# Attention probabilities turned by VectorE and DMA instead of TensorE, and weighed two tiles later

## What is computed

```python
xn = layernorm(x)                                   # x: (2, 1024, 512)
q, k, v = xn @ Wq.T, xn @ Wk.T, xn @ Wv.T           # 32 heads of q, 8 of k and v, 128 wide
q, k = rmsnorm(q, q_norm_w), rmsnorm(k, k_norm_w)
scores = q @ k.T / sqrt(128) + slope[head] * (key - query), -1e30 where key > query
s = (softmax(scores) @ v) @ Wo.T
g = silu((silu(xn @ w_gate.T) * (xn @ w_up.T)) @ w_down.T)   # 1376 inner columns
out = x + s * g
```

## Time and profile before

| | before |
|---|---|
| median of 3 runs | 2454.9 us (2453.91 to 2457.38) |
| the profiled execution: its time | 2455.46 us |
| the profiled execution: its span | 2453.7 us |
| TensorE busy | 99% of the span |
| VectorE, ScalarE, GpSimd busy | 69%, 50%, 31% |
| DMA moved | 92.19 MB, mean 38 GB/s |
| mean granted clock of TensorE | 0.998 of full speed |

### The profile page before, as it was taken

One profiled execution on the slowest core, in us unless ns is written; L12 is line 12 of the kernel. 1 busy time (PEld: TensorE's weight loads), 2 busy tenths in 40 slices (PEclk: granted clock), 3 DMA queues, 4 the chain that ended last, 5 costly groups with the idle time before them and its releaser, 6 DMA issues.

```text
span 2453.7 us, 37432 instructions
## 1 busy us (share of the span) xinstructions
PE 2422.6 (99%) x13232; PEld 2070.7 (84%) x13232; DVE 1693.7 (69%) x3788; ACT 1236.1 (50%) x2548; POOL 756.9 (31%) x2053
## 2 busy tenths in 40 slices
PE   7999999999999999999999999999999999999998
PEld 6888888888888888878888888888888888888887
DVE  7777777777778787823377787777777777777132
ACT  4555554555545555543355555555555545545333
POOL 2323231413233323244522232323232314131443
PEclk9999999999999999999999999999999999999999
DMA  3010000000000000023320101010000000010232
GB/s 130 1 40 4 27 18 27 18 27 18 27 18 27 18 27 18 27 91 125 112 78 1 44 1 44 1 44 1 27 18 26 18 27 18 1 44 14 90 103 103
DMA packets 23289, 92.19 MB, mean 38 GB/s; under 512 B 6592, under 2 KB 6720, under 8 KB 19136
## 3 DMA queue, kind: packets, MB, share of 16 engines
q1 hardware_dynamic: 23104, 89.80, 10.5%
HBM read 85.60 MB, written 4.19 MB: 37 GB/s over the span
## 4 chain that ended last, share of the span: by engine, by line
PE 96%; DVE 2%; ACT 1%; issue 1%; POOL 0%; DMA 0%; DVEq 0%; ACTq 0%; POOLq 0%
PE out_ps L401 17%; PE score_ps L377 16%; PE out_ps L414 14%; PE qkv_ps L351 14%; PE ring_ps L388 10%; PE qkv_ps L352 7%; PE score_ps L504 5%; PE qkv_ps L504 4%; PE ring_ps L520 4%; PE ring_ps L359 2%; PE out_ps L520 1%; PE ring_ps L364 1%; PE score_ps L351 0%; DVE y L997 0%; DVE xT_lo L868 0%
## 5 line engine op out<-in xcount | busy, mean ns | idle before, releaser
L597 ACT ACTIVATE pT_hi<-ring_ps 128x512 fp32r<-128x512 f32 x576 | 344.0, 599 | 509.8 <-PE ring_ps L388 497.2
L818 DVE TENSOR_TENSOR pT_lo<-ring_ps,pT_hi 128x512 fp32r<-128x512 f32 x576 | 396.8, 690 | 90.6 <-ACT pT_hi L597 86.0
L589 ACT ACTIVATE probs<-probs,low_min 128x896 f32<-128x896 f32 (+7 forms) x512 | 395.2, 774 | 50.4 <-DVE low_min L810 50.1
L1016 POOL TENSOR_SCALAR rs_x<-sq_sum 128x5 f32<-128x5 f32 x122 | 24.8, 203 | 1128.1 <-DVE sq_sum L749 1128.1
L388 PE MATMUL ring_ps<-ident,probs 128*128 128x128 f32 x2304 | 345.6, 273 | 0.0
L388 PEld LDWEIGHTS ring_ps<-ident,probs 128*128 128x128 f32 x2304 | 281.7, 140 | 42.1
L810 DVE CUSTOM_DVE_ANT_0 probs<-score_ps,rel_sb,slope 128x512 f32<-128x512 f32 (+5 forms) x504 | 301.7, 599 | 5.7 <-PE score_ps L377 4.3
L377 PE MATMUL score_ps<-kv_hi,qT_hi 128*128 128x320 f32 (+4 forms) x760 | 275.6, 363 | 3.0 <-DVE xT_lo L868 2.0
L401 PE MATMUL out_ps<-pT_hi,kv_hi 128*128 128x512 f32 x576 | 265.8, 461 | 2.9 <-DVE pT_lo L818 2.6
L377 PE MATMUL score_ps<-kv_hi,qT_lo 128*128 128x320 f32 (+4 forms) x760 | 261.0, 343 | 0.0
L377 PE MATMUL score_ps<-kv_lo,qT_hi 128*128 128x320 f32 (+4 forms) x760 | 260.3, 342 | 0.0
(11 more groups left out here) (178 smaller groups left out, 5293.5 us busy)
## 6 DMA issues: line engine op xcount, KB each, us to landing
qkv_raw<-w_ffn_dram SPq DMA_DIRECT2D x44, 768.0 KB, 4.2
qkv_raw<-w_qkv_dram SPq DMA_DIRECT2D x15, 1536.0 KB, 6.9
o_raw<-w_o_dram SPq DMA_DIRECT2D x16, 1024.0 KB, 4.8
o_raw<-x_dram SPq DMA_DIRECT2D x4, 1024.0 KB, 6.7
out_dram<-y SPq DMA_DIRECT2D x16, 256.0 KB, 3.7
probs<-x_dram SPq DMA_DIRECT2D x3, 1024.0 KB, 7.9
qkv_raw<-w_qkv_dram SPq DMA_DIRECT2D x4, 384.0 KB, 6.6
probs<-x_dram SPq DMA_DIRECT2D x2, 512.0 KB, 4.8
```

The lines of the kernel that those rows point to most:

```text
L589: act.activation(row, row, ACT.Exp, scale=-1.0, bias=low_min[:, i % 2, h, HEAD_CHUNKS[i] - 1:HEAD_CHUNKS[i]], accum_out=row_sum[:, i % 2, ...
L597: act.activation(pT_hi[:, n % SLOTS, :], ring_ps[:, ring_bank(r), :], ACT.Copy).then_inc(ring_high, 1)
L818: dve.tensor_tensor(out=pT_lo[:, n % SLOTS, :], in0=ring_ps[:, ring_bank(r), :], in1=pT_hi[:, n % SLOTS, :].bitcast(F32), op=ALU.subtract) ...
```

## The change

- The probabilities are no longer turned by TensorE. `turn_blocks` on VectorE turns them in place by blocks of 32x32 right behind the exponentials. SP writes the whole tile to a DRAM tensor (`turn_probs` on SP), waits until it is there, and reads it back (`probs_home`) by four DMAs for each group of up to four key tiles, each DMA filling 32 partitions, in runs of up to 2 KB. That places the blocks, so the tile arrives transposed in `pT`, which has two group buffers.
- There is one `probs` buffer (before: two), in an order by blocks of 32, so the first `bias` of a tile waits until the write of the previous tile has landed. `rel_sb` is laid out to match. The chunks of scores are now of 4 key tiles and the rest (before: equal halves), in three banks.
- The tile of queries i - 2 is weighed in step i, in one run after the scores, and its output is projected in step i + 1.
- `divide` is gone. The reciprocals travel through DRAM too (`rec_out_at`), come back as a row on all partitions, and `scale_att` (VectorE) multiplies the weighed output by them.
- `high_probs` and `low_probs` read SBUF instead of PSUM; 6 of the 36 low parts of a unit go to GpSimd (`POOL_LOWS`), and so does `low_att`, now with both inputs in SBUF.
- ScalarE squares and sums q and k in five instructions with accumulators (`squares`); VectorE's sum is gone.
- TensorE still turns q and k, into the bank that they were projected to. The scale of q and k is applied to k instead of q.
- SP's queue gets, for each tile, one write, the write of the reciprocals (4-byte pieces), the row's return, and four or eight DMAs back.

The core of the diff (the indentation is cut by 8; lines that only serve the first tiles are left out):

```diff
+GROUP = 4
...
+HIGH_SLOTS, LOW_SLOTS = 4, 3
+SBANKS = 3
...
+POOL_LOWS = {4: (2, 4), 5: (2, 4), 6: (3,), 7: (3,)}
...
-probs = [sb("probs0", [P, G, S - P]), sb("probs1", [P, G, S])]
...
+probs = sb("probs", [P, G * S])
+pT_hi, pT_lo = sb("pT_hi", [P, HIGH_SLOTS, G * P], F32R), sb("pT_lo", [P, LOW_SLOTS, G * P], F32R)
+pT, att = sb("pT", [P, 2, GROUP * G * P]), [sb("att0", [P, G * P]), sb("att1", [P, G * P])]
...
+turned_out = nc.dram_tensor("turned_out", (2, P, TILES * G * P), F32).ap()
+rec_out_at = nc.dram_tensor("rec_out_at", (2, G, P), F32).ap()
...
+def keys_of(i, part):
+    return part * GROUP, min((part + 1) * GROUP, i + 1)
...
+    def turn_probs(U, i):
+        t = tile(U, i)
+        slot = t % 2
+        alone(probs_turned, t * G)
+        if t > 2:
+            back = (U - (i < 2)) * GROUPS + GROUP_AT[(i - 2) % TILES + 1]
+            for k in range(2):
+                alone(probs_back[k], (back + 1 - k) // 2 * BLOCKS * 16)
+        sp.dma_start(turned_out[slot, :, 0:(i + 1) * G * P], probs[:, 0:(i + 1) * G * P]).then_inc(probs_out, 16)
+        alone(rec_done, t)
+        if t > 2:
+            alone(rec_back[slot], (t - 1) // 2 * 16)
+        sp.dma_start(rec_out_at[slot].rearrange("g p -> p g"), rec[:, i % 2, :], allow_slow_non_contiguous=True).then_inc(rec_out, 16)
+    def probs_home(U, i):
+        t = tile(U, i)
+        slot = t % 2
+        alone(probs_out, t * 16)
+        for part in range(GROUPS_IN[i]):
+            lo, hi = keys_of(i, part)
+            group = U * GROUPS + GROUP_AT[i] + part
+            if group >= 2:
+                done = chunks_to_group(group - 2)
+                alone(low_by_dve, done // TURNS * DVE_LOW_AT[TURNS] + DVE_LOW_AT[done % TURNS])
+                alone(low_by_pool, done // TURNS * POOL_LOW_AT[TURNS] + POOL_LOW_AT[done % TURNS])
+            there = turned_out[slot].rearrange("(a r) n -> r a n", a=BLOCKS)
+            run = (hi - lo) * G * SQUARE
+            for k in range(BLOCKS):
+                at = lo * G * P + k * run
+                sp.dma_start(pT[k * SQUARE:(k + 1) * SQUARE, group % 2, 0:BLOCKS * run]
+                             .rearrange("r (a n) -> r a n", a=BLOCKS), there[:, :, at:at + run]).then_inc(probs_back[group % 2], 16)
...
+    def rec_home(U, i):
+        t = tile(U, i)
+        slot = t % 2
+        alone(rec_out, t * 16)
+        if t > 2:
+            alone(att_split, t - 2)
+        sp.dma_start(att[i % 2][:, :], rec_out_at[slot:slot + 1].rearrange("a g p -> a (g p)").to_broadcast([P, G * P])
+                     ).then_inc(rec_back[slot], 16)
...
+        def attention(U, first, last):
+            for i in range(TILES):
+                loads(U, i, last)
+                if not (first and i == 0):
+                    rec_home(U - (i == 0), (i - 1) % TILES)
+                turn_probs(U, i)
+                if i == TILES - 3 and U + 1 < B * UNITS:
+                    alone(rq_done, (U + 1) * TILES)
+                    load_inv((U + 1) % UNITS)
+                if i == TILES - 1 and not last:
+                    load_slope((U + 1) % UNITS)
+                probs_home(U, i)
+                if last and i == TILES - 1:
+                    rec_home(U, i)
...
...
+        if not (first and n < SBANKS):
+            pe.wait_ge(biased, U * SCORES + n - SBANKS + 1)
+        k_hi, k_lo = k_by_block
+        for q, kt in ((qT_hi, k_hi), (qT_hi, k_lo), (qT_lo, k_hi)):
+            mm = pe.matmul(score_all[n % SBANKS][:, 0:(hi - lo) * P].rearrange("p (b j r) -> p b j r", b=BLOCKS, r=SQUARE),
+                           q[:, i % 2, h * P:(h + 1) * P], kt[:, :, lo:hi, :],
+                           start=(q is qT_hi and kt is k_hi), stop=(q is qT_lo))
...
-    def turn_probs(U, i, j, first):
-
-        r, p = RING_AT[i] + j, (i - 1) % TILES
-        ring_free(U, r, first)
-        for h in range(G):
-            if j == 0:
-                pe.wait_ge(divided, (U * TILES + i - 1) * G + h + 1)
-            tr = pe.transpose(ring_ps[:, ring_bank(r), h * P:(h + 1) * P],
-                              probs[p % 2][:, h, j * P:(j + 1) * P], ident[:, :])
-        tr.then_inc(ring_full, 1)
...
+        if not (last and i >= TILES - 2):
+            project(U + (i + 2) // TILES, (i + 2) % TILES, first and i + 2 < TILES)
+        if not (last and i >= TILES - 1):
+            turn_qk(U + (i + 1) // TILES, (i + 1) % TILES, first and i + 1 < TILES)
...
+        chunks = G * HEAD_CHUNKS[i] if i < TILES else 0
+        sooner = 2 if last and i == TILES - 2 else 0
+        for k in range(sooner):
+            scores(U, i, k, first)
+        if not (first and i <= LAG):
             out_project(U, i)
+        for k in range(sooner, chunks):
+            scores(U, i, k, first)
...
+        if not (first and i < LAG) and i < TILES + LAG:
+            V, p = U - (i < LAG), (i - LAG) % TILES
+            for j in range(p + 1):
+                weigh(V, p, j, None if first and i == LAG else U * TILES + i - LAG)
...
+    def squares(U, i, first):
...
+        for h in range(G + 1):
+            ins = act.activation(qk[i % 2][:, h * P:(h + 1) * P], acc[:, h * P:(h + 1) * P], ACT.Square,
+                                 accum_out=sq_sum[:, i % 2, h:h + 1])
+        ins.then_inc(summed, 1)
...
+            V, p = U - (i < LAG), (i - LAG) % TILES
+            highs = [] if i >= TILES + LAG or first and i < LAG else list(range(p + 1))
+            for j in highs[:HIGH_SLOTS]:
+                high_probs(V, p, j)
+            highs = highs[HIGH_SLOTS:]
+            N, n = U + (i + 1) // TILES, (i + 1) % TILES
+            if not (last and i >= TILES - 1):
+                high_q(N, n, first and n)
+                if n:
+                    high_k(N, n, first)
+            if not (last and i >= TILES - 2):
+                squares(U + (i + 2) // TILES, (i + 2) % TILES, first and i + 2 < TILES)
+                stage_v(U + (i + 2) // TILES, (i + 2) % TILES, first and i + 2 < TILES)
...
+            if i == TILES - 3 and U + 1 < B * UNITS:
+                act.wait_ge(qkv_in, (U + 1) * 16)
+                for c in range(DC):
+                    high_w(U + 1, c)
+            if i == LAG:
+                high_o(U, 0, not first)
+                high_o(U, 1, not first)
+            if i < TILES:
+                for h in range(G - 1):
+                    exp(U, i, h)
+                for j in highs[:1]:
+                    high_probs(V, p, j)
+                highs = highs[1:]
+                exp(U, i, G - 1)
+                if i == TILES - 1 and not last:
+                    high_k(U + 1, 0, False)
...
+            for j in highs:
+                high_probs(V, p, j)
...
-    def divide(U, i):
-
-        dve.wait_ge(exped, (U * TILES + i + 1) * G)
-        dve.reciprocal(rec[:, :], row_sum[:, i % 2, :]).then_inc(rec_done, 1)
-        dve.wait_ge(rec_done, U * TILES + i + 1)
-        for h in range(G):
-            row = probs[i % 2][:, h, 0:(i + 1) * P]
-            dve.tensor_scalar(row, row, rec[:, h:h + 1], None, ALU.mult).then_inc(divided, 1)
...
+    def turn_blocks(U, i, h):
+        dve.wait_ge(exped, (tile(U, i) - 1) * G + h + 1)
+        row = by_head[:, h, 0:(i + 1) * BLOCKS, :]
+        dve.transpose(row, row).then_inc(probs_turned, 1)
...
+    def scale_att(U, i):
+        t = U * TILES + i - LAG
+        dve.wait_ge(weighed, (t - 1) // TILES * TURNS + TURN_AT[(t - 1) % TILES + 1])
+        dve.wait_ge(rec_back[t % 2], ((t - 1) // 2 + 1) * 16)
+        scaled = att[(t - 1) % 2][:, :].rearrange("p (g a n) -> p g a n", g=G, a=BLOCKS)
+        dve.tensor_tensor(out=scaled, in0=out_ps[:, :].rearrange("p (a g n) -> p g a n", g=G, a=BLOCKS), in1=scaled,
+                          op=ALU.mult).then_inc(att_scaled, 1)
...
+            if not (first and i <= LAG):
+                scale_att(U, i)
+            N, n = U + (i + 1) // TILES, (i + 1) % TILES
+            if not (last and i >= TILES - 1) and not (first and i == 0):
+                scale_qk(N, n, first and n)
+            V, p = U - (i < LAG), (i - LAG) % TILES
+            lows = [] if i >= TILES + LAG or first and i < LAG else [j for j in range(p + 1) if not on_pool(p, j)]
+            for j in lows:
+                if j < LOW_SLOTS:
+                    low_probs(V, p, j)
+            lows = [j for j in lows if j >= LOW_SLOTS]
             if first and i == 0:
+                early_norms(tile(U, 2))
...
+            if not (last and i >= TILES - 1):
+                low_q(N, n, first and n)
+                if n:
+                    low_k(N, n, first)
+            chunks = G * HEAD_CHUNKS[i] if i < TILES else 0
+            sooner = 2 if last and i == TILES - 2 else 0
+            for k in range(sooner):
+                bias(U, i, k)
+            if not (first and i <= LAG):
+                if first and i == LAG + 1:
                     dve.wait_ge(y_free, b + 1)
+                    dve.memset(y[:, TILES - LAG - 1:TILES, :], 0.0).then_inc(y_zero, 1)
```

(41 more changed lines are left out.)

616 lines of the change are left out of this document (249 added, 367 removed).

## The result

| | before | after |
|---|---|---|
| median of the runs | 2454.4 us | 3357.1 us |
| profiled execution, span | 2453.7 us | 3349.5 us |
| one unit, the one shown | 127.7 us | 186.4 us |
| one unit, mean of six in the first row | 127.7 us | 183.6 us |
| TensorE busy, mean granted clock | 99%, 1.00 | 73%, 0.86 |

The changed kernel takes 1.369 times as long (95% interval 1.363 to 1.374). "Slower" was the likelier side of the forecast. Its 2505 us missed by 852 us, and the time is far outside the range.

The account below looks back on a forecast made before the run. TensorE alone was taken to set the pace (99% busy). Steps of 126.8 us plus 3.5 for the port give 130.3 a unit, 2.6 over 127.7; times 16 is 42, plus 8 for row ends: 2505 us, range 2370 to 2650.

Parts of the forecast that it names:

- first biases wait for the write: Step 7 of a unit: the previous tile's write lands at 9.7 us, first bias wanted 8.4, adding 1.3 us.
- step 3: Fourth step of a unit: output projection waits for GpSimd's low_att from 4.8 to 7.8 us; step takes 14.8 us.
- step 0: First step of a unit: 15.4 us, as a GpSimd low part stands behind the norms; this covers the write's delay.
- DMA: Transfers on SP's queue: 2.6 us for each MB plus 2.2 fixed, reciprocals counted as 0.26 MB coming back.
- Rival (2): Returns into 32 partitions run at half rate, 8.6 us a unit more, kernel 2643 us; chance 0.22.
- The port: VectorE and GpSimd block each other on two-SBUF-input instructions: 3.5 us a unit, between 0 and 8.
- The order in a step: TensorE stands for late VectorE and GpSimd work within steps 0 to 7 of a unit; steps sum to 126.8 us.
- rivals (1): VectorE's stretch is shorter, turns at the division's rate, no GpSimd blocking: unit 122.5 us, kernel 2380 us; chance 0.24.
- (3): A block turn on VectorE takes twice the assumed value: some 14 us a unit, kernel 2729 us; chance 0.06.
- TensorE's own work: TensorE's matmuls in a unit without the transposes of probabilities: 111.4 us, 16.2 us a unit removed.
- rival (4): The gain comes in full, with TensorE still the last to finish: kernel 2204 us; chance 0.05.
- Ends of a row: Extra time at the start and end of each of two rows: 4 us each, 8 in all.

Follow-up runs that it names:

- recT: Changed kernel, whole, with only the reciprocals turned on VectorE into rows and written in 16 pieces of 128 bytes: 2831.4 us.
- recT_free: Changed kernel with reciprocals as 128-byte rows, return order 0, 2, 1, 3, tile writes sourced from a never-overwritten buffer and VectorE's wait dropped: 2688.6 us.
- tinyT: Changed kernel with reciprocals as 128-byte rows, and each tile's write and returns cut to 128 bytes of each partition: 2588.4 us.
- quietT: `tinyT` with GpSimd's subtractions (low parts) made on an eighth of their columns: 2461.6 us.
- rec16: Changed kernel with reciprocals written to DRAM in 128 pieces of 16 bytes instead of 512 of 4, then read strided: 2906.8 us.
- rec16_wide: Changed kernel with 16-byte reciprocal pieces and each return filling all 128 partitions, block placement left out: 2793.2 us.
- noturnT: `quietT` with each VectorE turn cut to one block of 32 columns instead of a row: 2361.9 us.

## Why the prediction was wrong, by its own steps

The miss of 852 us, by differences of two kernels each, the later causes still in (16 units):

| step | the sum had | measured | from |
|---|---|---|---|
| reciprocals' trip | 0 beyond 0.26 MB | 526 us | after - `recT` |
| first biases wait for the write | 21 us (1.3 a unit) | 143 us (8.9) | `recT` - `recT_free` |
| the rest of the traffic (returns and slopes late) | 0 | 100 us (6.3) | `recT_free` - `tinyT` |
| GpSimd's subtractions, by the port or late | 56 us (3.5) and 48 us (3.0, step 3) | 127 us (7.9) | `tinyT` - `quietT` |

The four rows come to 896 us where the sum had 125, which is 771 of the 852. The other 82 are `quietT` against the 2380 us that the sum leaves without traffic, port and step 3's wait for GpSimd. (The sum has a delay by GpSimd in step 0 as well, not given by itself.)

**The step that failed.** "DMA", in its sentence "0.26 of reciprocals". I priced this transfer by its bytes, on its way home, and left its way out at nothing. 2 KB in 512 dense pieces is 62% of the miss. No row of the trace before has such pieces, so the term should have been bounded from both sides, as the turn's was. It was a cost of zero without a reason.

**Rival (2) was the right mechanism, too small a chance and incomplete.** "The returns run at half rate" is seen at 212 GB/s. Its price was 138 us over the forecast. The half rate by itself is worth 114 us (`rec16` - `rec16_wide`), and TensorE stands nearly as it said, 4.3 and 3.4 us ahead of the scores in a unit of `recT`. The sum's own 1.3 us for the first biases was too small besides. By its 2.6 us for each MB and 2.2 fixed, the 3.67 MB from -1.1 us on land at 10.6 and not at 9.7, which is a slip of 0.9 us a unit. The rival also left out two waits: the weighing two tiles behind waits for late returns, and the 2 KB of slopes queue behind a 2 MB write. I had written that in step 0 "the same delay is covered by GpSimd's low part"; the slopes' wait of 68 to 159 us shows that it isn't. My sign of it, "if the first biases wait several us for the write", came true: up to 12.6 us.

**The port** is there, its price isn't shown. The 480 low parts met GpSimd often enough to grow by 0.22 us on the mean, where the 36 of a unit before, with one input from PSUM, kept their 0.69. (In the earlier trace rows it was an instruction with one input from SBUF; `tinyT` against `quietT` shows it for two.) But TensorE's waits for them don't change, so the stretch of VectorE's low parts costs TensorE nothing that the waits show. I had counted 3.5 us a unit; the 7.9 of the table also hold step 3's wait, forecast as 3.0 and 2.74 in the trace, and a higher clock.

**The order in a step.** I had 126.8 + 3.5 - 1.3 = 129.0 us a unit without traffic; `tinyT` has 131.0. Without the port and step 3's wait I had 122.5; `quietT` has 123.9. Hand-counted steps were right to 2 us in sum, and TensorE waited where I had said, in a unit of `tinyT`:
```profile
PE out_ps L460 <- DVE pT_lo L872: 6.5, 4, 3.0
PE out_ps L472 <- POOL attT_lo L1134: 3.6, 2, 2.7
```
**The turn**: 1.2 us taken, 1.24 measured in the changed kernel, with 0.82 at 640 columns; the turn's rates of rivals (1) and (3) fall with it.
```profile
L847 DVE STREAM_TRANSPOSE probs<-probs 128x1024 f32<-128x1024 f32 x64 | 79.2, 1237 | 0.0
```
**TensorE's own work**: I subtracted 16.2 us a unit; `noturnT` still needs 118.7 against an expected 111.4. TensorE's busy time there is 115.8 (mean of six units), 11.8 less than before and not 16.2; the other 2.9 are idle. Which of its matmuls take the 4.4 us more stays open. So rival (4)'s 2204 us would not have come even with a turn that costs nothing.

**Ends of a row.** I put 8 us. In `tinyT` the first load of gate weights for a matmul is 50 us later than before (1103.7 against 1053.4 us). Its eight units account for 26 of these. Over the whole kernel, 2588.4 - 2454.4 = 134 us, less 16 x 3.3 = 53 for the units, leaves some 81 for the rows' starts and ends and the feed-forward parts between. Part of it lies at a row's start, for which I had 4 us together with its end: the slopes of the second unit are issued at 167.2 instead of 147.4 us, so the first unit alone is 20 us longer than before, where each of the next six is 3.4. Where the rest lies stays open.

**The clock** was no term of the sum. It is a consequence that adds to the waits: after a stand of several us the granted clock falls to 0.50 (693 to 695 us above), and TensorE's busy time in a unit, for the same matmuls (10928 in either kernel), is 115.8 us in `noturnT` at a clock of 0.99 and 127.8 in the change at 0.85 (means of six units). That is 12 of the 65 us between their units. No run of its own parts it from the waits.

## What to carry to other kernels

Give every transfer that a change adds, the smallest above all, a price of its own by its shape: bytes, pieces and what they share in DRAM, partitions reached, outermost dimension, and what is in flight beside it. A run with the same transfers but without their bytes parts the order of the steps from the traffic, here 2588 of 3357 us. A run that quiets one engine takes away that engine's own lateness together with what it does to others; what the critical engine waits for, before and after, tells which it was. A round trip to DRAM on one buffer needs more distance than "two tiles behind": the write must land before the next tile's first result, whatever the reader's lag.
